# Expert stages of a sixteen-stage hybrid model: token slots filled by indexed gathers, results scattered to token order, one block per stage

## The reference, cut to what matters

```python
eid = jnp.argmax(softmax(xf @ router_w + router_b), axis=-1)
rank = (jnp.cumsum(onehot, axis=0)[jnp.arange(N), eid] - 1.0).astype(jnp.int32)
valid = rank < C
buf = jnp.zeros((E, C, Dq)).at[eid, pos].add(xf * vmask)
h = relu(jnp.einsum('ecd,edh->ech', buf, w1) + b1[:, None, :])
y = jnp.einsum('ech,ehd->ecd', h, w2) + b2[:, None, :]
y_tok = y[eid, pos] * vmask
yov = relu(xf @ ow1 + ob1) @ ow2 + ob2
out = y_tok + yov * (1.0 - vmask)
```

## Time and profile before

| | us |
|---|---|
| median of 3 runs | 3220.36 (3217.41 to 3228.6) |
| the profiled execution | 3217.3 |
| its span | 3215.5 |
| first expert stage (layer 9), in the span | 1419.3 to 1526.4 |
| second expert stage (layer 11), in the span | 1711.05 to 1811.3 |

### The profile page before, as it was taken

How to read it: one execution, slowest core, us unless ns; L and a number is a source line. 1 busy time by engine, 2 the same in 40 slices (tenths; PEclk the granted TensorE clock), 3 DMA queues, 4 the chain that set the end, 5 groups by cost and what they waited for, 6 DMA issues and landing times. The chain is left out here.

```text
span 3215.5 us, 62100 instructions
## 1 busy us (share of the span) xinstructions
PE 2772.5 (86%) x24170; PEld 1821.1 (57%) x24194; DVE 1957.5 (61%) x4336; ACT 1402.4 (44%) x2938; POOL 1034.8 (32%) x1438
## 2 busy tenths in 40 slices
PE   6599799988799978876886799996999989889997
PEld 2234467756477755565454467764666656556664
DVE  4998754556555576642673366664666646556664
ACT  4455244434244435322452254453555534445553
POOL 1488432224233223213113333330222236312223
PEclk7799799999899988878997899999999999999999
DMA  1000100001000001010110000002122211112221
GB/s 75 1 1 1 54 1 1 1 18 31 4 1 1 1 1 44 8 70 19 24 28 19 11 1 1 1 1 64 56 69 80 63 30 29 56 47 67 71 80 45
DMA packets 50352, 94.56 MB, mean 29 GB/s; under 512 B 6516, under 2 KB 37036, under 8 KB 49296
## 3 DMA queue, kind: packets, MB, share of 16 engines
q1 hardware_dynamic: 48016, 89.97, 9.2%
q0 software_dynamic: 2048, 0.61, 0.1%
HBM read 71.60 MB, written 20.97 MB: 29 GB/s over the span
## 5 line engine op out<-in xcount | busy, mean ns | idle before, releaser
L566 ACT ACTIVATE s_sT<-s_R 128x1024 f32<-128x1024 f32 (+2 forms) x448 | 400.1, 945 | 199.6 <-PE s_R L500 198.7
L601 DVE TENSOR_REDUCE s_negm<-s_R 128x4 f32<-128x1024 f32 x320 | 377.0, 1220 | 154.1 <-PE s_R L471 154.0
L471 PE MATMUL s_R<-s_qk 32*128 32x256 f32 (+2 forms) x3584 | 241.8, 383 | 58.5 <-ACT s_sT L566 33.2
L500 PE MATMUL s_R<-s_qA,s_qk 32*128 32x256 f32 (+2 forms) x3584 | 240.5, 382 | 18.3 <-DVE s_negm L601 11.8
L573 ACT ACTIVATE s_oc<-s_OB 128x256 f32<-128x256 f32 x224 | 85.8, 383 | 339.5 <-PE s_OB L519 339.5
L519 PE MATMUL s_OB<-s_sT,s_v 128*32 128x256 f32 (+2 forms) x3584 | 225.2, 369 | 9.9 <-ACT s_sT L566 6.4
L471 PEld LDWEIGHTS s_R<-s_qk 32*128 32x128 f32 x3584 | 153.9, 185 | 106.6 <-issue 79.8
L616 DVE TENSOR_TENSOR s_qA<-s_qk,s_X 128x256 f32<-128x256 f32 x224 | 94.3, 421 | 194.9 <-PE s_X L531 194.9
L500 PEld LDWEIGHTS s_R<-s_qA,s_qk 32*128 32x128 f32 x3584 | 162.4, 184 | 79.6 <-issue 65.5
L1511 POOL TENSOR_TENSOR s_pr<-s_pr,s_rinv 128x1024 f32<-128x1024 f32 x64 | 121.1, 1892 | 218.3 <-DVE s_rinv L1619 218.3
L1591 ACT ACTIVATE s_pr<-s_S,s_negmax 128x256 f32<-128x256 f32 x256 | 118.5, 470 | 135.4 <-DVE s_negmax L1622 135.4
(11 more groups left out here) (593 smaller groups left out, 6264.4 us busy)
## 6 DMA issues: line engine op xcount, KB each, us to landing
s_wB<-enc_b SPq DMA_DIRECT2D x32, 962.5 KB, 4.7
s_scratch<-s_pk SPq DMA_DIRECT2D x58, 256.0 KB, 2.0
s_qk<-s_scratch SPq DMA_DIRECT2D x232, 64.0 KB
s_wA<-enc_a SPq DMA_DIRECT2D x32, 193.0 KB, 4.0
big<-moe SPq DMA_DIRECT2D x2, 2347.0 KB, 12.3
big<-routed SPq DMA_DIRECT2D x2, 2084.0 KB
all_W<-weights SPq DMA_DIRECT2D x1, 2104.0 KB, 15.3
all_W<-weights SPq DMA_DIRECT2D x1, 2103.5 KB, 10.8
```

The source lines that it names most:

```text
L471: last = pe.matmul(S[h][:, t * T:t * T + hi - lo], b.qk[rows, r % 2, 0, c, t * P:(t + 1) * P], b.qk[rows, r % 2, 1, c, lo:hi], start=(t == ...
L500: last = pe.matmul(b.R[:, a.turned_at(u, h // 2), :][:, h % 2, a.at(kt)], b.qk[rows, r % 2, 1, c, kt * P:(kt + 1) * P], b.qA[rows, u % 2, ...
L566: act.activation(b.sT[:, u % (a.lag + 1), 2 * p:2 * p + 2, 0:a.width], b.R[:, a.turned_at(u, p), 0:a.width], ACT.Exp).then_inc(s.expd, 1)
L601: ins = dve.tensor_reduce(b.negm[:, u % 2, :, at].rearrange("p t h -> p h t"), S.rearrange("p h (t k) -> p h t k", t=TT), AX_X, ALU.max, n ...
```

## The change

**In layer 8** (`kernel_attention_stage`) VectorE also takes the statistics of batch j-3 and scales batch j-4 in step j of its last loop, for six batches, and GpSimd runs `power_pool` for them. `LEFT` gets `"L2_attn_a": 6`, so layer 9 norms two batches.

**In both expert stages** routing and experts become one block:

- `sent` now holds the normed tokens in token order: SP stores the ready batches at once and the others when normed. The table of slots is turned round: instead of a slot for each token, a token for each slot. VectorE compares each token's rank with 256 values (`of_rank`, two operations of 2048 elements a lane, bf16 out); GpSimd multiplies the expert one-hot by tile number, row number and one (`places`); 32 bf16 matmuls of 128 x 24 add these up over the 16 tiles; eight small VectorE operations make row numbers of that, with an out-of-range number for empty slots. Slots 0 to 127 of each expert are one tile of 128, slots 128 to 159 of four experts together another, ten tiles in all.
- GpSimd gathers ten tiles from `sent` by those numbers into `rows`, each with its own semaphore, and scatters the ten tiles of results in five groups to `returned`, now in token order and zeroed before by SP. SP fetches `returned` back in four transfers of 256 KB when all ten have landed, and VectorE adds four tiles at a time.
- The order on TensorE: logits, wait for the weights (layer 9), hidden pieces of tokens 0 to 511, the two counting matmuls, hidden pieces of 512 to 1023, the table's matmuls, outputs 0 to 7, hidden pieces of 1024 to 1535, outputs 8 to 11, the turned rows, the experts, hidden pieces and outputs of 1536 to 2047.
- On VectorE eight of the `bias_own` stand ahead of the table's small operations, the other eight after outputs 0 to 7. ScalarE splits each expert's output in two activations. The weights get 312 more columns.

The diff, cut to its core:

```diff
+                    if 0 <= j - 3 < leave:
+                        dve.wait_ge(x_done, j - 2)
+                        nx.moments_dve(dve, g, j - 3)
+                    if 0 <= j - 4 < leave:
+                        nx.apply_dve(dve, g, j - 4)
...
+    taken = [[rest(0), main(0), main(1), main(2)], [main(3), rest(1), main(4), main(5)], [main(6), main(7)]]
+    given = [(1, [main(0), main(1)]), (3, [main(2), main(3), rest(0)]), (5, [main(4), main(5)]), (6, [main(6)]),
+             (7, [main(7), rest(1)])]
...
+            @block.sync
+                    sp.dma_start(g.BIG[:, half:width], g.a[which][:, half:width]).then_inc(loaded, 16)
+                    sp.dma_start(g.BIG[:, 0:half], g.a[which][:, 0:half]).then_inc(loaded, 16)
+                in_rows = sent.rearrange("(t p) d -> p t d", p=P)
+                if have:
+                    sp.dma_start(in_rows[:, 0:TT * have, :], g.h[:, 0:TT * have, :]).then_inc(stored, 16)
+                sp.wait_ge(ln.h_ready, B - have)
+                sp.dma_start(in_rows[:, TT * have:, :], g.h[:, TT * have:, :]).then_inc(stored, 16)
+                sp.wait_ge(back_zero, 1)
+                sp.dma_start(returned.rearrange("(t p) d -> p t d", p=P), back[:]).then_inc(returned_zero, 16)
+                sp.wait_ge(scattered, 16 * NB)
+                for k in range(4):
+                    sp.dma_start(back[:, 4 * k:4 * k + 4, :],
+                                 returned[4 * k * P:(4 * k + 4) * P, :].rearrange("(t p) d -> p t d", p=P))\
+                      .then_inc(fetched[k], 16)
...
+            @block.gpsimd
+                pool.tensor_tensor(places[:], onehot[:].unsqueeze(2).to_broadcast([P, NT, 3, E]), ...
+                pool.wait_ge(rows_zero, 1)
+                pool.wait_ge(stored, 32 if have else 16)
+                pool.wait_ge(indexed, 2)
+                for group in taken:
+                    for k in group:
+                        pool.indirect_dma_start(rows[:, k, :], None, sent,
+                                                bass.IndirectOffsetOnAxis(index[:, k:k + 1], 0),
+                                                bounds_check=NTOK - 1, oob_is_err=False).then_inc(gathered[k], 16)
+                pool.wait_ge(returned_zero, 16)
+                for n, (_, group) in enumerate(given):
+                    pool.wait_ge(yr_cp, n + 1)
+                    for k in group:
+                        pool.indirect_dma_start(returned, bass.IndirectOffsetOnAxis(index[:, k:k + 1], 0),
+                                                rows[:, k, :], None, bounds_check=NTOK - 1, oob_is_err=False)\
+                            .then_inc(scattered, 16)
...
+            @block.tensor
+                last.then_inc(logits, 1)
+                if big is not None:
+                    pe.wait_ge(loaded, 32)
+                hidden_own(0)
+                pe.wait_ge(onehot_ready, 1)
+                pe.matmul(CU, g.causal01[:, 0:P], oh, start=True, stop=True)
+                pe.matmul(TO, g.ones[:], oh, start=True, stop=True).then_inc(counted, 1)
+                hidden_own(1)
+                pe.wait_ge(placed, 1)
+                for h in range(2):
+                    pe.wait_ge(ranked, h + 1)
+                    for t in range(8 * h, 8 * h + 8):
+                        pe.matmul(YT[:, 0, 0:3 * E], of_rank[:, t, 0:P], of, start=(t == 0), stop=(t == NT - 1))
+                        last = pe.matmul(YT[:, 1, 0:3 * E], of_rank[:, t, P:], of, start=(t == 0), stop=(t == NT - 1))
+                last.then_inc(at_done, 1)
+                for t in range(8):
+                    outputs(t)
+                hidden_own(2)
+                for t in range(8, 12):
+                    outputs(t)
+                for n in range(len(taken)):
+                    turn_rows(n)
...
+            @block.scalar
+                        act.activation(yT[:, e - 1, :], YT[:, (e - 1) % 2, 0:P], ACT.Identity, bias=b2[:, e - 1:e])
+                        act.activation(yT[:, rest((e - 1) // 4), q * REST:(q + 1) * REST], YT[:, (e - 1) % 2, P:CAP],
+                                       ACT.Identity, bias=b2[:, e - 1:e]).then_inc(y_cp, 1)
...
+            @block.vector
+                for h in range(2):
+                    tiles = slice(8 * h, 8 * h + 8)
+                    dve.tensor_tensor(of_rank[:, tiles, :], g.w("moe_ranks").unsqueeze(1).to_broadcast([P, 8, 2 * P]),
+                                      rank[:, tiles].unsqueeze(2).to_broadcast([P, 8, 2 * P]), ALU.is_equal)\
+                       .then_inc(ranked, 1)
+                d.done(dve.tensor_scalar(inv[:], rank[:], float(CAP), None, ALU.is_gt))
+                if big is not None:
+                    dve.wait_ge(loaded, 32)
+                for t in range(8):
+                    bias_own(t)
+                dve.wait_ge(at_done, 1)
...
+                dve.tensor_copy(index[:, 0:E], at[:, 0, :]).then_inc(indexed, 1)
+                d.done(dve.tensor_tensor(none[:, 1, :], at[:, 1, :], g.w("moe_quarter"), ALU.mult))
+                d.done(dve.tensor_reduce(at_rest[:], none[:, 1, :].rearrange("p (k q) -> p k q", k=2), AX_X, ALU.add))
+                dve.tensor_copy(index[:, E:NB], at_rest[:]).then_inc(indexed, 1)
+                for t in range(8):
+                    add_own(t)
+                for t in range(8, NT):
+                    bias_own(t)
+                for t in range(8, 12):
+                    add_own(t)
```

538 lines of the change are left out of this document (262 added, 276 removed).

## The result

The changed kernel takes 3192.38 us in the median (3189.61 to 3195.48, four runs). The kernel before, run beside it, takes 3219.36 (3217.41 to 3228.6). The ratio is 0.9914 [0.9894, 0.9934], so 27.0 us less, between 21 and 34. The forecast was 3186 and the range 3171 to 3203.

What follows compares the result with a forecast made beforehand. Indirect DMAs bound two places in each expert stage, leaving TensorE idle. First use -18.2 plus 7.3 for the norm, second -20.4: together -31.3 from 3217.3, giving 3186 us; own range 3180 to 3192, with rivals A and B 3171 to 3203.

Steps and rivals of the forecast that it cites:

- The norm: Six batches normed in layer 8 add 7.3 us there; nothing saved in the first expert stage, where weights are late.
- One-hots: Rank one-hots on VectorE, two operations of 2048 elements: 2.34 us each, 4.7 together, at single rate.
- Rival A: More gained: one-hots at 1.2 us, no stall, second activation hidden, fetch 5.0; 5.7 us a stage, 3175; 22%.
- The stall beside the bias operations: Gathers slowed while VectorE runs eight more bias operations: bounds 0 and 2.0 us, 0.8 taken.
- Rival C: Slower: indirect DMAs take 3.01 us, not 0.97; 33 us a stage, 66 in all, 3252; 4%.
- The gathers' chain: Ten gathers on GpSimd's queue before the experts: 14.0 us, then 0.8 stall and 0.9 for last transposes and copy.
- TensorE's own order does not come last: Before the experts, TensorE's outputs and hidden pieces end at about 48 us, ahead of the experts' start at 51.0.
- only 1 to 2 us: TensorE's wait before the experts, short enough that it should enter them at the upper clock.
- Second activation: Splitting each expert's output on ScalarE adds 0.2 us per expert, 1.6 in all, not hidden.
- The end: Experts' start to next stage: 37.9 us, with last of three scatters starting at 28.3 and fetch taking 6.0.
- as much: TensorE's work in the first use of the expert stage, put equal to the second's 67.1 us.
- No other stage changes: Stages outside layer 8 and the two expert stages stay the same; the 312 added columns load under the first stage.

Runs made afterwards that it cites:

- a_no_norm: Changed kernel with the norm of six batches taken out of layer 8 and left in the first expert stage; 3192.30 us.
- a_bf16_rank: Changed kernel with both inputs of the rank one-hots in bf16 instead of f32; 3190.56 us.
- a_groups: Changed kernel with the scatters in six groups instead of five, expert 4's results scattered by themselves; 3186.30 us.
- a_again: The changed kernel run again with no edit, on another chip than its first profile; 3189.50 us.
- a_own_back: Changed kernel with the own network's third quarter (hidden pieces, outputs 8 to 11) back behind the experts; 3200.32 us.
- b_columns: Kernel before with only the 312 added weight columns, which nothing reads; 3231.17 us, against 3228.68 for the kernel before in the same session.
- a_bias_later: Changed kernel with VectorE's first eight bias operations behind the index table instead of ahead of it; 3192.20 us.
- a_table_first: Changed kernel without the moved norm, counting matmuls first, six scatter groups, and table matmuls ahead of own tokens 512 to 1023; 3179.28 us, 0.9856 of before.
- a_count_first: Changed kernel with the two counting matmuls ahead of the own network's first pieces and the wait for the weights; 3185.95 us.

## Why the prediction was right, step by step

The direction, the size (27 us against 31, with -31.3 inside the measured interval of -34 to -21) and the place were right. For the three stages, over two profiles of the kernel before (271.4 and 273.6) and three of the new code (241.9, 246.3 and, with the bf16 inputs that made no difference, 238.9), the change is -30.1 us, and -31.3 with the second barrier of each expert stage of before. That this is the forecast to a tenth is luck: the three sums alone differ by 7 us.

The steps of the first use, from its first instruction (1434.94), each with its own length in brackets:

| step | predicted | measured |
|---|---|---|
| weights landed, own network starts | 17.3 | 16.4 |
| first 512 tokens | 23.0 (5.7) | 21.5 (5.2) |
| counted | 23.9 (0.9) | 22.2 (0.6) |
| rank | 26.1 (2.2) | 24.4 (2.2) |
| two one-hots | 30.8 (4.7) | 28.8 (4.5) |
| threshold, eight bias operations | 33.1 (2.35) | 31.1 (2.3) |
| table | 34.7 (1.6) | 32.4 (1.3) |
| first gather | 35.3 (0.6) | 33.4 (1.0) |
| experts start | 51.0 (15.7) | 49.2 (15.8) |
| last expert out | 24.2 after that | 23.5 |
| last scatter begins | 28.3 | 28.9 |
| fetch issued | 30.4 | 31.0 |
| last addition ended | 37.1 | 37.6 |
| next stage | 37.9 | 38.6 |

- **The norm: the size right, the judgement of its use right.** From the last operation ahead of layer 8's loop to the next stage it took 16.9 us and now 22.6, so 5.7 more (predicted 7.3); the whole layer took 8.3 more between the two first profiles, and 5.3 between the means over all. Its saving in the expert stage was put at nothing in the first use, and `a_no_norm` shows a little less than nothing.
- **One-hots: right**, 2.29 us each against 2.34. Rival A's 1.2 is out, and `a_bf16_rank` shows that types alone don't give it.
- **The stall beside the bias operations: near its lower bound.** The two gathers beside them in the second use took 1.11 and 1.27 us instead of 1.00, so 0.4 in all, and one in the first use 1.12, where 0.8 was taken. Rival C (3.01 us each) didn't occur: of the 40 indirect DMAs none took over 1.32.
- **The gathers' chain: right in sum, incomplete as a reason.** 15.7 was predicted for the step to the experts and 15.8 measured. The sentence "TensorE's own order does not come last" holds to 0.5 us in the first use and fails in the second use of this profile: the gathers started 1.7 us earlier than forecast (24.5 against 26.2), the experts 0.5 later (42.4 against 41.9). `a_groups` and `a_bf16_rank` have the two level in both uses, `a_again` and `a_no_norm` have TensorE last in both, so the code alone doesn't decide which comes last, and that the first use came out right is in part luck. I had TensorE wait "only 1 to 2 us", and had moved the second use's path earlier by the 9.6 us of the weights without doing TensorE's sum again. Around the one-hots TensorE has this stretch there, 3.3 us idle:

```profile
1720.00:1730.00 10.00, 6.71 (x56) 4.33 (x55) 9.44 (x25) 2.64 (x4) 0.00 (x0) 0.87 0.01 2
```

- **Second activation: half of the term.** An expert takes 2.81 to 2.82 us instead of 2.71 to 2.72, so 0.7 in eight, not 1.6; rival A had it at nothing.
- **The end: right, by two errors that nearly cancel.** The last expert was out 0.7 earlier, but five scatters stood in a row where I had counted three, since GpSimd waited for a group of two (1507.86) and had three more behind it; `a_groups` takes 1.5 us of that back. The fetch took 6.5 us to the last addition, 6.7 predicted.
- **A reading.** The prediction has TensorE work "as much" in the first use as the 67.1 us of the second; the rows of its six stretches add up to 70.7. No term of the sum uses it.
- **What no run separates.** The change also merges two blocks, which takes two barriers out of each use, and brings ten indirect DMAs each way for sixteen. Only the place of the own network's third quarter was undone by itself (`a_own_back`, 7.4 and 5.3 of the some 19 us); how the rest divides is read from the steps, not shown by an edit.
- **What the sum left out** is the noise of the other stages. "No other stage changes" was right of the code (`b_columns`), but two profiles of one code differ by 5 us in layer 0 alone. The 4 us between 27.0 and 31.3 are within the interval, and I can't assign them.

## What to carry to other kernels

When data is moved by many small indirect DMAs on one queue, count the items and look what work of another engine could lie beside them: here 10 gathers of 1.30 us with 14 us of matmuls beside them beat 16 scatters, a load and 10 us of idle TensorE. After such a fill, do TensorE's sum again for each use of the stage; once it is last, an earlier table or fewer operations ahead of it give nothing (`a_bias_later`, `a_table_first`), and only taking a wait out of its queue does (`a_count_first`). A norm that is moved under another stage is for the most part paid where that stage's own engine sets the pace (5.7 of 7.3 us here), and saves nothing if a load is late next. And where an addition seems to wait for a DMA, look in the DMA records when its packets ended, and at the instruction ahead of it, before the DMA is blamed.

## What the runs showed of the hardware

- TensorE's clock falls at other moments in each execution of the same code: layer 0 took 81.0 to 86.4 us, with the mean granted clock between 0.67 and 0.60. A difference of one profile in a stage that isn't touched needs a second profile before it is explained.
- In four kernels that ran on one chip VectorE began additions up to 8.3 us after TensorE had ended their inputs, beside GpSimd's indirect DMAs; on the other chip the same instructions began after 0.11 us. The gathers' packets ended as early on both. The cause was not found.
- The 3.01 us scatter is no accident. It was the second scatter of the second use in each of the four profiles of the kernel before and its two altered copies, each time beside the sixteen bias operations (1725.77 to 1730.06 in the first profile; the scatter 1727.89 to 1730.90). Beside the bursts of eight of the changed code nothing like it appeared, and no indirect DMA of its variants took over 1.5 us. The Trainium skill (SBUF — State Buffer, A bandwidth-pool intuition that's wrong) tells of a DMA issued by GpSimd beside a VectorE copy that takes some 3100 ns, blocked until about 115 ns after VectorE's end. Here the duration agrees, but the scatter ended 0.84 us after the burst, the one before it lay wholly inside the burst and took 1.10, and in the first use, where the same burst ran from 1441.44 to 1445.73, the scatters from 1442.23 on took 1.27 at most. So at most one DMA of a burst fits the rule, and not its 115 ns; what singles it out was not settled.
- Matmuls of 24 bf16 columns follow each other at 25 ns: the 16 of the table's first half started between 1461.72 and 1462.10, 0.4 us where 1.8 was allowed for. The Trainium skill (TensorE: Matmul & The Clock Gate) gives 25 ns as the least distance of two matmuls; the trace agrees.
